# Attention stage: the turns of the probabilities ahead of the pieces of neighbouring batches

## What is computed

```python
qkv = x @ w_qkv                      # 32 heads of 16, 8 key/value heads
xq, xk = _apply_rope(xq), _apply_rope(xk)
scores = einsum('bhsd,bhtd->bhst', xq, keys) * scale      # causal mask
probs = softmax(scores)
out = einsum('bhst,bhtd->bhsd', probs, values)
return out.reshape(bs, seq, 512) @ w_o
```

## Time and profile before

| | |
|---|---|
| median of 3 runs | 1904.93 us (1902.29 to 1907.94) |
| the profiled execution | 1906.81 us, its span 1905.0 us |
| TensorE busy | 1666.1 us |
| VectorE, ScalarE, GpSimd busy | 1037.7, 793.0, 601.3 us |
| mean granted clock of TensorE | 0.953 |
| slot 0 to slot 191 of the attention stage | from about 1303 to about 1852 us of the span |

### The profile page before, as it was taken

How to read it: one execution, slowest core, us unless ns; L and a number is a source line. 1 busy time by engine, 2 the same in 40 slices (tenths; PEclk the granted TensorE clock), 3 DMA queues, 4 the chain that set the end, 5 groups by cost and what they waited for, 6 DMA issues and landing times. The chain is left out here.

```text
span 1905.0 us, 25873 instructions
## 1 busy us (share of the span) xinstructions
PE 1666.1 (87%) x8965; PEld 1393.2 (73%) x8965; DVE 1037.7 (54%) x2013; ACT 793.0 (42%) x1603; POOL 601.3 (32%) x792
## 2 busy tenths in 40 slices
PE   5999986999999999999999998028889889899884
PEld 4899874888888888778778887026778778777763
DVE  7888755522232226753433234755767767767772
ACT  4676643222122112212212111406867776776760
POOL 5454551211111113431111134124344444444422
PEclk9999997999999999999999999558999999999996
DMA  4000002000011012310110001200000000000000
GB/s 134 13 23 12 1 1 78 23 23 21 25 34 31 23 35 75 103 59 15 34 37 27 21 23 44 76 1 1 1 1 12 12 1 12 12 1 13 12 7 18
DMA packets 28548, 52.16 MB, mean 27 GB/s; under 512 B 3520, under 2 KB 4704, under 8 KB 28416
## 3 DMA queue, kind: packets, MB, share of 16 engines
q1 hardware_dynamic: 28416, 50.47, 8.5%
HBM read 42.07 MB, written 8.39 MB: 26 GB/s over the span
## 5 line engine op out<-in xcount | busy, mean ns | idle before, releaser
L1171 POOL TENSOR_TENSOR m_a_lo<-m_prod,m_a_hi 128x512 fp32r<-128x512 f32 x100 | 130.8, 1308 | 640.3 <-ACT m_a_hi L1229 640.2
L1345 DVE TENSOR_TENSOR m_prod<-m_prod,m_ps 128x512 f32<-128x512 f32 x100 | 68.8, 688 | 482.0 <-ACT m_prod L1225 481.9
L114 PE MATMUL m_ps<-m_hT_hi,m_w_hi 128*128 128x512 f32 x800 | 317.8, 397 | 7.5 <-DVE m_w_lo L1327 5.3
L116 PE MATMUL m_ps<-m_hT_hi,m_w_lo 128*128 128x512 f32 x800 | 317.7, 397 | 0.0
L115 PE MATMUL m_ps<-m_hT_lo,m_w_hi 128*128 128x512 f32 x800 | 317.1, 396 | 0.0
L1225 ACT ACTIVATE m_prod<-m_ps 128x512 f32<-128x512 f32 x100 | 59.7, 597 | 577.9 <-PE m_ps L116 577.9
L1802 ACT ACTIVATE t_p<-t_ps,t_nmax 128x128 f32<-128x128 f32 (+1 forms) x512 | 181.0, 424 | 75.0 <-DVE t_nmax L1924 74.8
L1924 DVE TENSOR_REDUCE t_nmax<-t_ps 128x2 f32<-128x512 f32 (+1 forms) x192 | 132.0, 688 | 96.6 <-PE t_ps L1993 60.1
L114 PEld LDWEIGHTS m_ps<-m_hT_hi,m_w_hi 128*128 128x128 f32 x800 | 151.3, 189 | 44.1 <-issue 5.7
L115 PEld LDWEIGHTS m_ps<-m_hT_lo,m_w_hi 128*128 128x128 f32 x800 | 151.2, 189 | 36.3
L116 PEld LDWEIGHTS m_ps<-m_hT_hi,m_w_lo 128*128 128x128 f32 x800 | 151.0, 189 | 36.4
(11 more groups left out here) (259 smaller groups left out, 3732.4 us busy)
## 6 DMA issues: line engine op xcount, KB each, us to landing
m_raw<-in_w_mlp SPq DMA_DIRECT2D x75, 256.0 KB, 2.7
a_xt<-in_x SPq DMA_DIRECT2D x8, 512.0 KB, 3.8
m_old<-in_x SPq DMA_DIRECT2D x16, 256.0 KB, 4.2
x_store<-stream SPq DMA_DIRECT2D x4, 1024.0 KB, 5.1
m_old<-x_store SPq DMA_DIRECT2D x16, 256.0 KB, 2.7
out<-t_yl SPq DMA_DIRECT2D x16, 256.0 KB, 2.0
q_raw<-in_w_attn SPq DMA_DIRECT2D x10, 256.0 KB, 5.1
a_att<-in_w_mixer SPq DMA_DIRECT2D x8, 256.0 KB, 2.8
```

What stands on the lines that cost most here:

```text
L114: pe.matmul(out, w_hi, x_hi, start=first, stop=False)
L116: return pe.matmul(out, w_lo, x_hi, start=False, stop=last)
L1171: pool.tensor_tensor(a_lo[:, n % 2, :], prod[:, :], f(a_hi[:, n % 2, :]), ALU.subtract).then_inc(lo, 1)
L1345: dve.tensor_tensor(prod[:, :], prod[:, :], ps[:, U + TURN_AT["unit", n, 0] % 2, :], ALU.mult).then_inc(prodd, 1)
```

## The change

In each slot the turns of unit s are issued right behind the values of unit s-2, ahead of the slot's pieces, where before they were issued behind them. The lists of the other engines stay as they are.

```diff
@@ -2096,6 +2096,8 @@
                     scores(s + 1)
                 if 0 <= s - 2 < SLOTS:
                     values(s - 2)
+                if 0 <= s < SLOTS:
+                    transposes(s)
                 for what, part, t, b in JOBS[s]:
                     job = name_of(what, part, t, b)
                     if what not in HALVED or part == 0:
@@ -2108,8 +2110,6 @@
                         stack(what, part, t, b, bank_of(job))
                     else:
                         project(what, part, t, b, bank_of(job))
-                if 0 <= s < SLOTS:
-                    transposes(s)
 
         @block.sync
         def _(sp):
```

## The result

| | before | after |
|---|---|---|
| median | 1904.13 us, 20 runs (1900.17 to 1907.94) | 1898.57 us, 20 runs (1896.28 to 1901.39) |
| span of the profiled execution | 1905.0 us | 1896.2 us |
| start of the span to the first mask of the attention stage | 1302.88 us | 1301.37 us |
| first to last mask of the stage (units 0 and 191) | 542.57 us | 535.27 us |
| behind it | 59.6 us | 59.6 us |

What follows compares the result with a forecast made beforehand. The stage was taken as a loop of four engines with TensorE the fullest. Five periods of 1.37 us (6.85), 0.4 and 1.86 at the edges gave 9.1 us off 1904.93: 1895.8 us, range 1887 to 1903.5.

Steps and rivals of the forecast that it cites:

- the walk: One attention batch followed slot by slot, each engine in written order: 1.37 us gained of a 3.96 us ceiling; chance 0.56.
- effect (b): In slots without a stall, pieces end 0.44 us later, so their ScalarE and VectorE drains, next maximum and exponentials come later.
- Effect (c): Turns need their exponentials by the end of the values, 0.35 us to spare in slot 55; no wait unless exponentials slip.
- the rival with a chance of 0.10: Softmax late in slots 1, 17, 18 and 19: turns wait once exponentials slip over 0.35 us; 12.3 us slower, 1917; chance 0.10.
- Batch of 70.9: Sign that the walk is right: an attention batch takes about 70.9 us instead of 72.2.
- Values' waits larger: Sign that the walk is right: TensorE's waits of the values, 12.1 us before, get not smaller but rather larger.
- No waits of the turns: Sign that the walk is right: the turns hardly ever wait for exponentials on TensorE.
- Turned tiles' waits "about 19": Sign that the walk is right: TensorE's waits for turned tiles fall from 23.7 to about 19 us.
- from its stalls I take 0.4: Gain assumed for the first period, which has few pieces of a batch before: 0.4 us, bounds 0 and 1.37.
- get as far as slot 22's -0.93 each: The period into the last batch and the last batch itself gain 0.93 us each: 1.86, bounds 0 and 2.74.
- The tail: Behind the last slot, turns come 1.39 us earlier, but their low part stands behind VectorE's biased output: nothing more gained.
- A clock rival: Clock falls to 1.2 GHz in the stretch of slots 64 to 66: 5.8 us a batch, 35 in six, 1931; chance 0.02.

Runs made afterwards that it cites:

- e7: Kernel before, with the turns ahead of the pieces in slots 15, 16 and 17 of a batch alone: 1907.02 us, ratio 1.0012 to before.
- e9: Kernel before, with the turns ahead of the pieces in slot 22 of a batch alone: 1900.72 us in one run, period 71.75 us.
- e5: Changed kernel, with the turns behind the pieces again in slots 4 and 5 of a batch alone: 1895.19 us, ratio 0.9947 to before.
- e3: Changed kernel, with the turns one step further ahead, before the values of unit s-2: 1897.38 us, ratio 0.9963 to before.
- e2: Changed kernel, with the turns ahead only in the fifteen slots of a batch where no piece stalls: 1916.64 us, ratio 1.006 to before.
- e6: e1, with the high part of the turned probabilities ahead of the slot's drains on ScalarE: 1917.88 us, ratio 1.0069 to before.
- e1: Changed kernel, with the turns ahead only in the nine stalling slots (1, 2, 7, 10, 15, 17, 18, 19, 22): 1890.58 us, ratio 0.9929 to before.

## Why the prediction was right, and where its size was not

**The batch, slot by slot: right.** Offsets of the kernel after against before at the end of a slot, batch 3 and the start of batch 4, counted, as in the walk, from the end of slot 2 (the mask of unit 76):

| end of slot | 7 | 10 | 15 | 16 | 18 | 19 | 22 | 2 |
|---|---|---|---|---|---|---|---|---|
| walked | -0.04 | -0.30 | -0.44 | 0 | -0.45 | -0.67 | -0.93 | -1.37 |
| measured | -0.04 | -0.34 | -0.47 | -0.03 | -0.47 | -0.65 | -0.92 | -1.33 |

No place is off by more than 0.04 us. Slot 7 loses its fill to late drains, as walked, though half a step earlier and by another operand: the values there already take 0.59 us from their mask instead of 0.15, because their low part stands behind the late maximum on VectorE. The walk had let only the turned tile wait. Slots 16 and 18 give back, slots 10, 19, 22 and 1 keep. e7 and e9 show the two kinds alone, and e5 shows effect (b) alone.

**Effect (c), the softmax: right that it costs nothing.** The smallest slack measured in the repeating batches was 0.22 us, in slot 15, and the next 0.33, in slot 18; the turns never waited there. Slot 7 had 0.36, against 0.35 in the prediction, which had not named slot 15 among the tight ones. e3 then took the slack away altogether, and the period didn't move. So the rival with a chance of 0.10, had it come, would have had the wrong price.

**What it would show.** Batch of 70.9: 70.86. Values' waits larger: 20.8. No waits of the turns: one. Turned tiles' waits "about 19": 13.8. That figure set the gain of 1.37 a batch against the waits, but a stall that holds the turns is counted as idle only for the rest, whether or not its 0.44 us comes back elsewhere.

**The sum: where it was too large.** The range held, but the forecast gain was 9.1 us, and the profile shows 7.3 from the first mask to the last:

| part | forecast | measured |
|---|---|---|
| unit 0 to 28 | -0.4 | +0.46 |
| five periods, to unit 148 | -6.85 | -6.62 |
| to unit 172 | -0.93 | -1.10 |
| to unit 191 | -0.93 | -0.04 |
| behind | 0 | 0 |

The terms that were mis-sized are "from its stalls I take 0.4" and, for the last batch, "get as far as slot 22's -0.93 each": the two edge batches. They were not walked but priced like the middle. In slot 0 the turns waited 1.2 us for the exponentials with a piece ahead of them; now they wait 1.7 and the piece stands behind, which makes that slot 0.43 us longer. Slot 11 of the first batch is another 0.43 longer: its values wait 0.21 us for a low part, where they didn't wait before. And in the last batch the values of slot 183 wait for their low part. Before:
```profile
1828.07 0.38 PE L2026 MATMUL t_ps<-t_pT_hi,t_v 128*128 128x256 f32 x1 [0.45 <-DVE t_pT_lo L1930]
```
after:
```profile
1819.90 0.39 PE L2026 MATMUL t_ps<-t_pT_hi,t_v 128*128 128x256 f32 x1 [0.87 <-DVE t_pT_lo L1930]
```
That is the exchange of slot 16 once more: 0.42 of a filling given back. Slot 172 does the same: the wait of its values grows from 0.40 to 0.83 us. That this comes of the smaller number of pieces in the edge batches, with less of TensorE's own work between two waits, is likely but not shown. The two terms make up the error of 1.8 us (0.86 and 0.89); the other two miss by 0.23 and 0.17 in opposite directions.

The tail was right: nothing is gained behind the last mask. After the last slot the low part starts right behind the biased output, as the prediction had it, in the timeline of VectorE:
```profile
1843.11 0.69 DVE L1893 TENSOR_TENSOR t_yl<-t_ps,f_bias 128x512 f32<-128x512 f32 x1 [2.16 <-PE t_ps L116]
1843.71 0.68 DVE L1930 TENSOR_TENSOR t_pT_lo<-t_ps,t_pT_hi 128x512 fp32r<-128x512 f32 x1
```
Before, it had waited another 0.37 us for its high part. So the values of unit 191 do start 0.22 us earlier, counted from their mask, but at the end of the span these are gone again (59.6 us in both). What takes them was not traced.

**Left open.** The profile's stage lost 7.3 us, in two profiled executions of the kernel after against one of the kernel before, and the medians 5.6 and 5.8, with intervals that reach to 7.0 and 7.6. Between kernels the two measures differ by up to 3.4 us (e2: stage 8.3 more, median 11.7 more; e6: 14.2 and 12.4; e1: 13.7 and 14.3 less). The stages ahead spread over 5 us, what stands behind over 58.3 to 60.8 us. Which of the two carries the last 1.6 us was not measured.

**What the walk left on the table.** It counted the gain of the change as given. That slots without a stall paid for it was in the walk (slot 7's loss), but the conclusion was not drawn: moving nothing there, as in e1, makes the batch another 0.79 us shorter and the time another 8.0 us.

## What to carry to other kernels

In this kernel, filling a stall of an in-order engine paid only where the next wait in its list was for something that the engine itself starts earlier now; where it was for another engine's queue, the filling came back as a longer wait there, in full. Look for the next wait before you fill a stall. Each piece of work pushed back to fill a stall delays what others drain from it, so move it in the slots that stall and leave the rest: of the 2.1 us a batch that the nine stalls of this kernel gave, 0.8 went again through slots that had none. Judge by the distance between equal instructions of two iterations, not by totals of waits, and walk the first and the last iteration for themselves.

## What the runs showed of the hardware

**The clock can fall within such a loop.** The prediction gave the clock a chance of 0.02 in the change, and in the profiled executions of all kernels here but two the granted clock was 1.00 throughout the repeating batches. In e7 it fell once, at the end of slot 18 of batch 3, and in e6 once, in slot 7 of batch 6. The stretches around e7's fall, by stretch as in the earlier trace rows; the first and third are the same 5 us of two batches in a row:
```profile
1556.00:1561.00 5.00, 3.10 (x18) 2.23 (x19) 2.96 (x7) 4.95 (x12) 1.02 (x4) 1.00 0.00 0
1562.00:1563.00 1.00, 1.00 (x6) 0.90 (x6) 0.20 (x1) 1.00 (x3) 0.72 (x2) 0.50 0.02 8
...
1628.99:1633.99 5.00, 3.07 (x18) 2.21 (x19) 2.96 (x7) 4.96 (x12) 1.00 (x4) 1.00 0.00 0
```
A clock of 0.50 is the lower of its two levels, 1.2 GHz of 2.4. Ahead of it TensorE had been busy for 3.10 of 5.00 us, with two stalls of 0.83 and 0.81; a batch later the same stretch, at 3.07 of 5.00, was followed by no fall. A 256-column matmul that starts 0.12 us behind the last one at the full clock took 0.21 there:
```profile
1562.34 0.41 PE L1998 MATMUL t_ps<-t_mask,t_id_r 128*128 128x256 f32 x1
1562.56 0.41 PE L2026 MATMUL t_ps<-t_pT_hi,t_v 128*128 128x256 f32 x1
```
It lasted some 3 us, in which TensorE worked without a break, and that batch took 72.99 us instead of 72.15: 0.84 us, not the 5.8 that the prediction had priced for a whole stretch of 11.4 us at the lower clock. A clock rival of this kind is possible here at about 0.8 us a time; 6 to 7 us if it came in each of the eight batches is an estimate from that one case. What tells a stretch that is followed by a fall from its twin that isn't, these runs don't show.
